# A transformer block with routed experts: one pass over both choices, with adding scatters, in place of two passes through a table of pairs

## The reference

```python
x = x + attention(layernorm(x), ...)                  # 4 x 2048 tokens, C = 256
xf = layernorm(x)
logits = xf @ Wr + br                                 # 8 experts
topk_w, topk_idx = top_k(logits, 2)
topk_w = softmax(topk_w)                              # two shares for each token
h = relu(xf @ W1[e] + b1[e])                          # 256 -> 512
y = h @ W2[e] + b2[e]                                 # 512 -> 256
x = x + sum over the two chosen e of share_e * y_e
```

## Time and profile before

| | us |
|---|---|
| median of three runs | 2733.09 |
| lowest and highest | 2732.42, 2741.71 |
| span of the profiled execution (the only time that it has) | 2735.5 |
| `mix`, to the last scatter of the list | about 1942 to 2185 |
| `experts`, to the end | 2186 to 2735.5 |

### The profile page before, as it was taken

The page is one execution under the profiler, slowest core; times in us unless marked ns, Lnnn a source line. Parts: engine busy times, 40 slices in busy tenths (PEclk is TensorE's granted clock), DMA queues, the critical chain, the costliest instruction groups (busy, mean ns, idle before and its releaser), DMA issues. The chain is left out here.

```text
span 2735.5 us, 48214 instructions
## 1 busy us (share of the span) xinstructions
PE 2406.9 (88%) x15842; PEld 1359.7 (50%) x15842; DVE 2048.1 (75%) x5002; ACT 1581.1 (58%) x2716; POOL 823.7 (30%) x1130
## 2 busy tenths in 40 slices
PE   6885799999999999999999999998777389998998
PEld 6774333333334333333334333332444278887897
DVE  3876989998999898888898998940355457765776
ACT  3663277777777776667777777776433234433443
POOL 1543011211212112111212112121055655555554
PEclk8997699999999999989999999997888689999999
DMA  3777814414504513504414423010675323323332
GB/s 145 261 260 212 113 39 63 74 42 61 86 29 64 86 34 59 84 27 65 83 35 64 80 44 71 8 31 20 236 203 177 94 92 113 107 93 96 111 109 72
DMA packets 147501, 255.95 MB, mean 94 GB/s; under 512 B 72951, under 2 KB 91897, under 8 KB 138916
## 3 DMA queue, kind: packets, MB, share of 16 engines
q1 hardware_dynamic: 114544, 164.96, 27.1%
q0 software_dynamic: 29904, 80.65, 8.9%
q10 hardware_dynamic: 2812, 7.26, 1.5%
HBM read 147.59 MB, written 107.76 MB: 93 GB/s over the span
## 5 line engine op out<-in xcount | busy, mean ns | idle before, releaser
L836 ACT ACTIVATE prob<-ps_s 128x512 f32<-128x512 f32 (+5 forms) x1620 | 1078.1, 714 | 480.5 <-PE ps_s L932 477.8
L857 DVE TENSOR_REDUCE maxes<-ps_m 128x2 f32<-128x1024 f32 x768 | 913.9, 1221 | 107.8 <-PE ps_m L973 104.8
L932 PE MATMUL ps_s<-q_st,k_st 50*128 50x512 f32 (+3 forms) x2560 | 610.2, 413 | 73.8 <-ACT prob L836 57.2
L973 PE MATMUL ps_m<-k_st,q_st 48*128 48x512 f32 (+3 forms) x2560 | 603.2, 443 | 75.9 <-DVE maxes L857 39.6
L953 PE MATMUL ps_o<-prob,v_sb 128*17 128x512 f32 (+3 forms) x5120 | 617.5, 556 | 1.2 <-ACT prob L836 0.7
L802 POOL TENSOR_SCALAR_AFFINE_SELECT prob<-prob 128x256 f32<-128x256 f32 x512 | 203.2, 406 | 1347.8 <-ACT prob L836 1220.8
L973 PEld LDWEIGHTS ps_m<-k_st,q_st 48*128 48x128 f32 x2560 | 272.6, 191 | 531.3 <-DVE maxes L857 256.6
L861 DVE CUSTOM_DVE_ANT_0 junk<-ps_m,causal 128x128 f32<-128x128 f32 (+3 forms) x1024 | 453.1, 484 | 44.2 <-PE ps_m L973 42.7
L932 PEld LDWEIGHTS ps_s<-q_st,k_st 50*128 50x128 f32 x2560 | 318.3, 190 | 306.1 <-ACT prob L836 234.1
L1728 ACT ACTIVATE h_hi<-ps_turned 128x512 fp32r<-128x512 f32 x142 | 85.0, 598 | 225.6 <-PE ps_turned L1843 157.9
L94 PE MATMUL ps_out<-experts_hi,h_lo 128*128 (+1 forms) x568 | 173.0, 305 | 0.0
(11 more groups left out here) (187 smaller groups left out, 3180.6 us busy)
## 6 DMA issues: line engine op xcount, KB each, us to landing
parts_dram<-parts SPq DMA_DIRECT2D x64, 512.0 KB, 3.8
q_st<-parts_dram SPq DMA_DIRECT2D x84, 256.0 KB, 8.5
k_st<-parts_dram SPq DMA_DIRECT2D x84, 256.0 KB, 18.4
v_dram<-v_out SPq DMA_DIRECT2D x16, 544.0 KB, 5.5
xin<-in_L_attn_x SPq DMA_DIRECT2D x16, 512.0 KB, 6.0
ffn_raw<-in_L_ffn_W POOLq DMA_DIRECT2D x32, 256.0 KB, 5.2
y_dram<-y_sb SPq DMA_DIRECT2D x64, 128.0 KB, 2.0
split_hi<-ffn_hi POOLq DMA_DIRECT2D x16, 512.0 KB, 3.2
```

The lines of the kernel that those rows point to most:

```text
L836: last_exp = nc.scalar.activation(prob[:, at:at + n, lo:TB], bank[:, 0:n, lo:TB], ACT.Exp, scale=DH ** -0.5)
L857: return nc.vector.tensor_reduce(maxes[:, 2 * pair:2 * pair + 2, qt, kc], bank[:, :, :], AX.X, ALU.max)
L932: mm = nc.tensor.matmul(ps_s[k % 2][:, i, lo:TB], k_st[half(h % 2, ROWS), w % BUFS, h // 2, kt * P:(kt + 1) * P], q_st[half(h % 2, ROWS), ...
L973: mm = nc.tensor.matmul(ps_m[slot][:, i, 0:wide], q_st[half(i, STACK), w % BUFS, pair, qt * P:(qt + 1) * P], k_st[half(i, STACK), w % BUFS ...
```

## The change

The pairs are no longer split by choice. The list has one region for each expert, with entries of 8 bytes (row number and share), and both choices of a token go there. The largest number of tiles for 16384 pairs and 8 experts is 135.

`mix` stores two things for each block: `x1` straight to the output, and the normalised rows to `rows_dram`, which it had made for the router anyway. The second store waits for ACT's normalised rows and stands on SP's queue ahead of the loads; ACT in turn waits for the store of two blocks earlier. DVE gets one operation more (`both`, the two one-hot tables summed for the counting) and loses two copies of scale and shift; the counting tables have half the width.

`experts` gathers normalised rows, so that ACT's L1718 is gone and PE turns the gathered rows directly. The result, bias added, is multiplied by the share on ACT (`share_out`) in place of DVE's L1781, into the gathered buffer. POOL then issues a scatter that adds to the output (`compute_op=ALU.add`). As a token stands in two tiles, and two adds to one row must not overlap, each of these scatters waits until the one before it has landed.

```diff
-PASS_TILES = (B * T + E * (P - 1)) // P
-TILE_COUNT = TOP * PASS_TILES
+TILE_COUNT = (TOP * B * T + E * (P - 1)) // P
-WORDS = 4
+WORDS = 2
@@ mix, SP
+            def store_rows(n):
+                sp.wait_ge(xn_made, n + 1)
+                sp.dma_start(rows_v[n, :, :, :], xn[:, n % 2, :, :]).then_inc(rows_stored[n % 2], 16)
...
-                sp.dma_start(rows_v[n, :, :, :], x1[:, n % 2, :, :]).then_inc(rows_stored[n % 2], 16)
+                sp.dma_start(out_v[n, :, :, :], x1[:, n % 2, :, :]).then_inc(x1_stored[n % 2], 16)
+                if n >= 1:
+                    store_rows(n - 1)
@@ mix, ACT, normalise
+                    act.wait_ge(rows_stored[n % 2], 16 * (n // 2))
@@ mix, DVE
+                    tt(out=both[:, m % 2, :, :], in0=hot[:, m % 2, :, 0, :], in1=hot[:, m % 2, :, 1, :],
+                       op=ALU.add).then_inc(hot_made, 1)
...
-                    for word, values in ((2, rstd), (3, shift)):
-                        nc.vector.tensor_copy(entry[:, here, :, word].bitcast(F32),
-                                              values[:, n % 2, :].unsqueeze(2).broadcast_to([P, TILES, TOP]))
@@ experts, POOL
-            def scatter(s):
-                pool.wait_ge(z_made, s + 1)
-                to, lo = (pairs_dram, 0) if s < PASS_TILES else (out_v, C)
...
+            def add_to_out(s):
+                if s:
+                    pool.wait_ge(scattered[(s - 1) % ROWBUFS], 16 * ((s - 1) // ROWBUFS + 1))
+                pool.wait_ge(z_made, s + 1)
+                pool.indirect_dma_start(out_v[:, :], bass.IndirectOffsetOnAxis(ap=lists[:, s % LISTS, 0:1], axis=0),
+                                        rows[:, s % ROWBUFS, :], None, bounds_check=B * T - 1, oob_is_err=False,
+                                        compute_op=ALU.add).then_inc(scattered[s % ROWBUFS], 16)
...
             for s in range(TILE_COUNT):
-                scatter(s)
...
-                if s == PASS_TILES - 1:
-                    for u in range(ROWBUFS):
-                        pool.wait_ge(scattered[u], 16 * len(range(u, PASS_TILES, ROWBUFS)))
-                    for ahead in range(PASS_TILES, PASS_TILES + EARLY_ROWS):
-                        gather_second_half(ahead)
+                add_to_out(s)
+                if s + ROWBUFS - 1 < TILE_COUNT:
+                    gather(s + ROWBUFS - 1)
@@ experts, ACT
-                if s + 4 < TILE_COUNT:
-                    normalise(s + 4)
...
+            def share_out(s):
+                act.wait_ge(list_in[s % LISTS // 2], lists_landed(s))
+                act.wait_ge(y_made, s + 1)
+                nc.scalar.activation(rows[:, s % ROWBUFS, :], y[:, s % YBUFS, :], ACT.Identity,
+                                     scale=lists[:, s % LISTS, 1:2].bitcast(F32)).then_inc(z_made, 1)
@@ experts, PE
-                pe.wait_ge(xn_made, s + 1)
+                pe.wait_ge(gathered[s % ROWBUFS], 16 * (s // ROWBUFS + 1))
```

More of the change, by code:

```diff
@@ L1236, in _ @@
                 last = nc.vector.memset(rank[:, e:e + 1], float(E - e))
-            for i in range(TOP):
-                for e in range(E):
-                    last = nc.vector.memset(run[:, 0, i, e:e + 1], float((i * E + e) * REGION))
+            for e in range(E):
+                last = nc.vector.memset(run[:, 0, e:e + 1], float(e * REGION))
             setup.done(last)
@@ L1521, in tiles_by_expert @@
     nc.vector.memset(clipped[:, TILE_COUNT:TILE_COUNT + 3], 0.0)
[L1522 to L1527, removed]
+    nc.vector.tensor_copy(clipped[:, 0:E], numbers[:, 0:E])
+    for e in range(E):
+        last = ts(own[:, e:e + 1], counts[:, e:e + 1], float(-e * REGION - 1), 0.0, ALU.add, ALU.max)
     steps.done(last)
-    steps.done(nc.vector.tensor_copy(whole_i[:, :, :], own[:, :, :]))
-    steps.done(ts(whole_i[:, :, :], whole_i[:, :, :], P.bit_length() - 1, None, ALU.logical_shift_right))
-    steps.done(nc.vector.tensor_copy(tiles[:, :, :], whole_i[:, :, :]))
+    steps.done(nc.vector.tensor_copy(whole_i[:, :], own[:, :]))
+    steps.done(ts(whole_i[:, :], whole_i[:, :], P.bit_length() - 1, None, ALU.logical_shift_right))
+    steps.done(nc.vector.tensor_copy(tiles[:, :], whole_i[:, :]))
     end, at, d = tiles, 0, 1
@@ L1534, in tiles_by_expert @@
         new = ends[at]
-        nc.vector.tensor_copy(new[:, :, 0:d], end[:, :, 0:d])
-        steps.done(tt(out=new[:, :, d:E], in0=end[:, :, d:E], in1=end[:, :, 0:E - d], op=ALU.add))
+        nc.vector.tensor_copy(new[:, 0:d], end[:, 0:d])
+        steps.done(tt(out=new[:, d:E], in0=end[:, d:E], in1=end[:, 0:E - d], op=ALU.add))
         end, at, d = new, 1 - at, 2 * d
@@ L1539, in tiles_by_expert @@
     number = numbers[:, 0:MORE]
[L1540 to L1555, removed]
+    here = slice(E, TILE_COUNT)
+    steps.done(tt(out=passed[:, :, :], in0=number.unsqueeze(2).broadcast_to(table),
+                  in1=end[:, :].unsqueeze(1).broadcast_to(table), op=ALU.is_ge))
+    steps.done(nc.vector.tensor_reduce(expert[:, :], passed[:, :, :], AX.X, ALU.add))
+    steps.done(tt(out=passed[:, :, :], in0=passed[:, :, :],
+                  in1=tiles[:, :].unsqueeze(1).broadcast_to(table), op=ALU.mult))
+    steps.done(nc.vector.tensor_reduce(skipped[:, :], passed[:, :, :], AX.X, ALU.add))
+    ts(clipped[:, here], expert[:, :], float(E - 1), None, ALU.min)
+    steps.done(tt(out=skipped[:, :], in0=number, in1=skipped[:, :], op=ALU.subtract))
+    steps.done(ts(skipped[:, :], skipped[:, :], float(P), float(P), ALU.mult, ALU.add))
+    steps.done(stt(out=row_of[:, here], in0=expert[:, :], scalar=float(REGION), in1=skipped[:, :],
+                   op0=ALU.mult, op1=ALU.add))
     nxt = [clipped[:, i:i + TILE_COUNT] for i in range(4)]
@@ L1563, with lists_landed, experts @@
 ROWBUFS = 12
[L1564 to L1577, removed]
+YBUFS = 2
+MORE = TILE_COUNT - E
+def lists_landed(s):
+    alone = 1 if s % 2 == 0 and s == TILE_COUNT - 1 else 0
+    return 32 * (s // LISTS + 1) - 16 * alone
+def experts(nc, block, slots_made, listed_rows, w_sb, numbers, counts, entry, slots, biases, biases_in, rows_dram, list_dram, out):
     w_hi, w_lo = w_sb
```

151 lines of the change are left out of this document (46 added, 105 removed).

## The result

| us | median | lowest | highest | runs |
|---|---|---|---|---|
| before, run beside it | 2732.76 | 2720.63 | 2741.71 | 4 |
| changed kernel | 2864.59 | 2853.38 | 2892.87 | 4 |

The change makes the kernel slower: 1.0495 of the time before, interval 1.0421 to 1.0568. The forecast was 2748, with a range up to 2807. The profiled execution has a span of 2853.9 us, of which the forecast of the same kind is 2750.4 (2748 and the 2.4 of before), so 103.5 us are to be found.

A forecast was written before the change was run, and what follows sets the result against it. PE was taken to bound the kernel before, and the loop of adds the changed one: 2217.3 us plus 134 periods of 3.96 us gives 2748 us, with an 8-in-10 range of 2690 to 2807.

The forecast's parts named there:

- The loop of adds: Scatters of `experts`: each add waits for the last one's landing, 3.11 us plus wake-up and second wait, 3.96 us a tile.
- the 4.46 of its own text: Add loop in `experts` if the destination's read is a third piece in POOL's issue, 0.5 us more.
- Wake-up: POOL in the add loop starts 0.82 us after what it waited for, plus 0.03 for the second wait instruction.
- PE's sum: If PE's loop decides: span 2735.5 - 24.7 - 11.1 - 0.6 - 3 = 2696.1, time 2694 us.
- 24.7, 11.1 and 3: Savings in `experts`, in us: seven fewer tiles, no wait at the change of choice, no two-tile lag at the end.
- `mix`: Stage storing 512 KB more for each of 16 blocks: zero change in time, between -10 and +10 us.
- The first, hidden adds: In `experts`, adds hide behind PE's loop, period up to 3.60, time 2694, up to 2700 us; chance 0.26.
- The second, reading and writing one after the other: Adds in `experts` read, then write: period 5.11, 2902 us; chance 0.12, together with all above 4.45.
- The third, `mix` longer by 26 us: Stores lengthen each of 16 `mix` blocks by 1.6 us, 26 us on rival 1: 2720; chance 0.04.
- The fourth, ACT as the pace: ACT sets the tile's pace in `experts`, 0.1 us more a tile on rival 1: 2707; chance 0.04.
- sign of being wrong: In the add loop: landing within 2.7 us of the start, or POOL going on sooner than 0.8 us after landing.
- The loop of 3.57: Add loop by the collectives rule alone, adding only a second source read: 3.27 + 0.30 us, time that of rival 1.

## Why the prediction was wrong

The mechanism that it forecast is the one that came. The size of one term failed.

**The loop of adds, the step that failed.** The prediction put the loop at 3.96 us; the typical one is 4.61 and the mean 4.703. By its terms:

| term | forecast | measured |
|---|---|---|
| POOL's issue, part of the landing | 1.01 | 1.59 |
| from its end to the landing | 2.10 | 3.79 - 1.59 = 2.20 |
| wake-up and second wait | 0.85 | 0.82 |
| typical loop | 3.96 | 4.61 |

"That POOL's issue of 1.01 us stays is my choice" is the sentence that was wrong: 0.58 us x 134 = 78 us of the 103.5. The prediction had named the other value, 1.5, with a loop of 4.46, and rested its number on 1.01 because the earlier trace rows shows plain scatters and gathers alike at 1.0; but no row showed an adding one, and the chosen value stood at the cheap end. The flight was off by 0.10 (13 us). Its two parts, 0.30 for as many bytes again and 0.36 for reading DRAM, are not how it is made up, for the flight of adds scales at 0.5 us for 64 KB, where plain ones took 0.25 for 128 KB more; the sum came near all the same. The mean's 4.70 against 4.61 is 12 us, and the shorter wake-up takes 4 off. Together that is 134 x (4.703 - 3.96) = 99.6 us; the first add 1.7 us later and 2.3 us more behind the last start complete the 103.5.

**The range** ended at a loop of 4.4, so it left out the 4.46 of its own text, though even that, 2815, would not have held the result. Only the bound of 5.11 did, and the chances gave 0.12 to all above 4.45. With no row for the operation itself, the forecast was too sure of the sum of its near rows.

**Wake-up.** 0.82 forecast, with 0.03 for the second wait; 0.81 to 0.82 measured with both. Right, and needed: a loop of the landing alone, 3.8, would have left the kernel near the time before (3.85 by the prediction's own sum).

**PE's sum.** 2694 was forecast for hidden adds. The kernels with more than one add under way came to 2694.73, 2699.24 and 2692.40, and to gains of 39, 36 and 41 us over the 2733.74, 2734.98 and 2733.74 of before, against 39 forecast. The whole is right, but in part because misses cancel. From the first scatter to the last, two adds under way take 470.6 us and the kernel before 516.5, 45.9 less, where the forecast's terms for that stretch (24.7, 11.1 and 3) give 38.8. Behind the last start it takes 8.8 us where it took 5.8, and `mix` is longer, by 8 us in that profile. Of the terms only the tiles are shown by themselves (23.9 for 24.7).

**`mix`.** Forecast at zero, between -10 and +10; it is 5 to 12 us longer. That it ended within 10 us of 2185 (2184.9) was luck: in this profile it lasted 11.7 us longer and began 10.8 us earlier. The added store, the wait of ACT behind it and DVE's added operation all come into question; none was tried.

**The rivals.** The first, hidden adds, is false for this kernel and true for two under way. The second, reading and writing one after the other, needed 5.11; single loops reach that, the typical one does not. The third, `mix` longer by 26 us, did not come at that size, but its direction was right. The fourth, ACT as the pace, is out by the period of 3.51 with all of ACT's work in place.

**What would show it.** POOL's idle time ended by the DMA to `out`, PE waiting for rows at the turning, the chain over DMA: all came. The add landed in 3.8 us, above the 2.7, and POOL went on 0.81 to 0.82 us behind the landing, so neither sign of being wrong came; the adds' distance of 3.96 did not come either. The busy share of PE was to be 0.89 and is 0.81 to 0.85, as the loop is longer. The granted clock was 0.95 to 1.00 in the steady stretches, where it was 0.99 and 1.00 before.

**The Trainium skill's rules.** The measured add costs more than the Trainium skill's page "Collectives: The Full Stack", section "The bandwidth ceiling: the fold count and why AG ≠ RS ≠ AR", gives it. That section speaks of collectives in a ring, and for this form, a scatter that POOL issues, it is not half the rate in the DMA engines but under a third (16.6 us of engine time against 4.9), and 0.57 us on the issuing engine. The loop of 3.57 worked out from it was 1.0 too short. The range of 3.5 to 5.3 from the Trainium skill's page "DMA: Bandwidth & Descriptors", section "Latency and other measured facts", holds the 4.6; no run here tells how much of the flight is such an access.

**What stays open.** 16 of the 134 loops take over 5 us, and make the mean 0.09 longer than the typical one. They are not of one kind: from 2501.55 the landing took 5.03 us, and from 2507.40 it took 3.84, but POOL then stood for 1.26 us where it stands for 0.55 otherwise. What delays either was not tried. Why adding costs POOL a fixed half microsecond more was not tried either.

## What to carry to other kernels

Where an engine may issue a transfer only when the last has landed, the loop is issue, flight and wake-up together, here 1.6 + 2.2 + 0.8 us for 128 KB, and it has to be set against the bound of a tile before the change is made. If the loop is the longer one, look first for a second transfer that may be under way: here two adds at once took the whole loss back and turned 1.05 of the time into 0.985. And where an operation has not been seen in a trace, put the range's end at the dearest value that a mechanism gives, not at the one that looks like its neighbours. When the result is in, compare stages by their own length and not by where they end: an end can stand still because two shifts cancel.

## What the runs showed of the hardware

- An adding indirect scatter of 128 rows of 1 KB holds POOL for 1.59 us, a plain one for 1.02. Of these 0.57 us, 0.52 are there with 64 rows too.
- With the same bytes the page of the changed kernel counts 37472 packets in POOL's queue, and that of the plain variant 24512: 12960 more, 96 for each of 135 scatters. With adds of 64 rows it counts 28832, which is 8640 fewer, 64 for each: one packet for each row that is added. So an add goes as 128 packets, and the plain scatter of as many rows as 32. The comparison of half rows and half as many rows shows that it is not the number of packets that the flight goes by, but the bytes.
- From the landing to POOL's next start it takes 0.81 us, of which 0.76 (0.02 + 0.55 + 0.19) are a time in which POOL waits for nothing that the profile shows.
